# Unread matrix products in more idle gaps of TensorE, and the first half's rows of an attention loaded quad by quad

## The reference

```python
x = x + 0.5 * L0_ffn(layernorm(x))    # three trees of 16 leaves give q, k, v; then softmax(q k) v
x = x + L0_attn(layernorm(x))         # 16 causal heads of 8, rope, alibi
x = x + 0.5 * L0_ffn(layernorm(x))
x = x + 0.5 * L1_ffn(layernorm(x))    # 8 experts, top 2, and a shared one
x = x + L1_attn(layernorm(x))         # a state space block: conv, scan over 16 states, gate
x = x + 0.5 * L1_ffn(layernorm(x))
```

## Time and profile before

| | |
|---|---|
| median of three runs | 1326.98 us (1323.32, 1326.98, 1327.03) |
| profiled execution | 1324.17 us, its span 1322.4 us |
| PE busy | 1220.3 us, 92% of the span, 6083 products |
| DVE, ACT, POOL busy | 906.3, 641.6 and 241.4 us (69%, 49%, 18%) |
| chain that ended last | PE 72%, DVE 11%, ACT 9% |
| mean granted clock of PE | 0.989 of full speed |

### The profile page before, as it was taken

How to read it: one execution, slowest core, us unless ns; L and a number is a source line. 1 busy time by engine, 2 the same in 40 slices (tenths; PEclk the granted TensorE clock), 3 DMA queues, 4 the chain that set the end, 5 groups by cost and what they waited for, 6 DMA issues and landing times.

```text
span 1322.4 us, 17165 instructions
## 1 busy us (share of the span) xinstructions
PE 1220.3 (92%) x6083; PEld 784.8 (59%) x6132; DVE 906.3 (69%) x1754; ACT 641.6 (49%) x1188; POOL 241.4 (18%) x205
## 2 busy tenths in 40 slices
PE   5998788899899989899999969889998998999998
PEld 3676444567666555566667744346776665555665
DVE  6755867455467698986765677664555677889765
ACT  4544354544422597952234325454433227979222
POOL 3000100000020084751000010000000102938210
PEclk9999899999999999999999999999999999999999
DMA  6212220000101030320100032200001011212220
GB/s 231 57 33 80 56 76 19 2 1 1 64 1 64 4 118 23 116 81 1 73 25 1 24 89 54 63 3 0 1 1 64 16 50 58 81 58 80 65 72 9
DMA packets 33365, 63.27 MB, mean 48 GB/s; under 512 B 4384, under 2 KB 20096, under 8 KB 33088
## 3 DMA queue, kind: packets, MB, share of 16 engines
q1 hardware_dynamic: 33280, 62.17, 15.0%
HBM read 54.23 MB, written 8.45 MB: 47 GB/s over the span
## 4 chain that ended last, share of the span: by engine, by line
PE 72%; DVE 11%; ACT 9%; issue 3%; POOL 2%; DMA 2%; SPq 1%; another core or an unknown queue 0%; DVEq 0%; POOLq 0%; ACTq 0%
PE bank L1543 13%; PE bank L1545 13%; PE bank L1544 13%; PE bank L1722 9%; PE bank L1552 5%; DVE a_mx L1426 3%; ACT n_part L1093 3%; PE bank L1877 3%; PE bank L1621 3%; ACT n_da L1085 2%; PE bank L1787 2%; PE bank L1692 2%; POOL n_hc L840 2%; PE bank L1758 2%; PE bank L1826 1%
## 5 line engine op out<-in xcount | busy, mean ns | idle before, releaser
L1270 DVE SCALAR_TENSOR_TENSOR f_hl<-bank,f_hh 128x512 fp32r<-128x512 f32 x192 | 131.9, 689 | 130.4 <-ACT f_hh L914 129.6
L914 ACT ACTIVATE f_hh<-bank 128x512 fp32r<-128x512 f32 x192 | 115.0, 599 | 188.1 <-PE bank L1621 149.2
L980 ACT ACTIVATE m_sl<-bank 128x512 f32<-128x512 f32 x144 | 86.2, 599 | 235.4 <-PE bank L1545 233.4
L840 POOL TENSOR_TENSOR n_hc<-n_h,n_cs 128x512 f32<-128x512 f32 x128 | 160.7, 1287 | 35.3 <-DVE n_h L1514 31.1
L1543 PE MATMUL bank<-xT_h,mw_h 128*128 128x512 f32 x288 | 161.2, 560 | 3.5 <-DVEq L537 2.7
L1514 DVE TENSOR_TENSOR_SCAN n_h<-n_da,bank 128x512 f32<-128x512 f32 x128 | 149.1, 1206 | 5.1 <-PE bank L1552 2.3
L1722 PE MATMUL bank<-m_h,mw 128*128 128x512 f32 x288 | 145.6, 594 | 0.0
L1337 DVE TENSOR_TENSOR m_t<-m_sl,bank 128x512 f32<-128x512 f32 x128 | 87.9, 687 | 78.7 <-PE bank L1545 77.3
L1426 DVE TENSOR_REDUCE a_mx<-bank 128x1 f32<-128x384 f32 (+3 forms) x176 | 106.0, 638 | 39.8 <-PE bank L1828 37.4
L771 POOL TENSOR_TENSOR small<-small,half 128x4 f32<-128x4 f32 (+1 forms) x24 | 26.8, 1115 | 577.3 <-DVE small L1176 577.3
L1877 PE MATMUL bank<-n_hc,ident 128*128 128x512 f32 x256 | 131.0, 599 | 0.2
(11 more groups left out here) (248 smaller groups left out, 2331.1 us busy)
## 6 DMA issues: line engine op xcount, KB each, us to landing
n_cs<-c_dram SPq DMA_DIRECT2D x32, 512.0 KB, 3.6
m_c<-comb_dram SPq DMA_DIRECT2D x28, 512.0 KB, 5.2
stage_fw<-in_fw_dram SPq DMA_DIRECT2D x6, 512.0 KB, 6.4
stack_dram<-R SPq DMA_DIRECT2D x16, 192.0 KB, 2.8
w_stage<-in_mw_dram SPq DMA_DIRECT2D x9, 256.0 KB, 2.7
stack_dram<-R SPq DMA_DIRECT2D x16, 128.0 KB, 2.6
a_q<-stack_dram SPq DMA_DIRECT2D x4, 512.0 KB, 5.3
a_k<-stack_dram SPq DMA_DIRECT2D x8, 256.0 KB, 4.7
```

Source lines behind the costliest of these rows:

```text
L840: n_hcs.by(nc.gpsimd.tensor_tensor(n_hc[:, i % 4, :], n_h[:, i % 4, :], n_cs[:, j % C_RING, i // 2 % 2, :], ALU.mult))
L1270: f_lo.by(V.scalar_tensor_tensor(f_h[1][:, i % 4, :], bank[:, i % 3, :], 0.0, f_h[0][:, i % 4, :].bitcast(F32), ALU.max, ALU.subtract))
```

## The change

`keep_busy` gets the bank as an argument. `attend` gets a table: ahead of an item of the tail it makes that many unread products, into bank 1. `mha` makes unread products ahead of three jobs of the pair's first list. And the groups of rows become four, one for each quad, so that quads 0 and 1 are loaded and waited for by themselves.

```diff
+TAIL_IDLE = {("turn", 1): 7, ("turn", 2): 7, ("turn", 3): 3, ("weigh", 3): 7}
+FIRST_IDLE = {NS1 + 3: 3, NS1 + 5: 6, NS1 + 6: 15}
...
-        a_ldq = [sig(f"a_ldq_{n}", "mha", 1, 16) for n in range(3)]
-        a_ldk = [sig(f"a_ldk_{n}", "mha", 2, 16) for n in range(3)]
+        a_ldq = [sig(f"a_ldq_{n}", "mha", 1, 16) for n in range(QUADS)]
+        a_ldk = [sig(f"a_ldk_{n}", "mha", 2, 16) for n in range(QUADS)]
...
-                    for n in range(3):
+                    for n in range(QUADS):
                         sp.wait_ge(a_ldq[n].sem, a_ldq[n].at(k - 1, 0))
...
-                first, count = ((0, 4), (4, 2), (6, 2))[n]
+                first, count = 2 * n, 2
...
                         sp.wait_ge(unit_done, done_before(u))
-                        head_rows_in(k, 1)
                         head_rows_in(k, 2)
+                        head_rows_in(k, 3)
...
                             head_rows_in(k + 1, 0)
+                            head_rows_in(k + 1, 1)
...
                             sp.wait_ge(a_s2.sem, a_s2.at(k, 3 * STEPS_4 - 1))
-                            head_rows_in(k + 1, 1)
+                            head_rows_in(k + 1, 2)
...
                             sp.wait_ge(a_s2.sem, a_s2.at(k - 1, NS2 - 1))
-                            head_rows_in(k, 2)
+                            head_rows_in(k, 3)
...
                     head_rows_in(k, 0)
+                    head_rows_in(k, 1)
...
-                    attend(k, [item for at in sorted(ATTEND_AT) for item in ATTEND_AT[at]])
+                    attend(k, [item for at in sorted(ATTEND_AT) for item in ATTEND_AT[at]], TAIL_IDLE)
...
-            def attend(k, items):
+            def attend(k, items, idle={}):
                 for what, qt in items:
+                    keep_busy(idle.get((what, qt), 0), 1)
...
-                    for job, x, which in HEADS_PLAN[-1]:
+                    for n, (job, x, which) in enumerate(HEADS_PLAN[-1]):
+                        keep_busy(FIRST_IDLE.get(n, 0), 1)
                         head_job(k, job, which)
...
-                pe.wait_ge(a_fill.sem, a_fill.at(k // 2, 1 if n == 0 else 3))
+                pe.wait_ge(a_fill.sem, a_fill.at(k // 2, 1 if n < 2 else 3))
...
-                    if n % NS1 == 0 and quad != 1:
-                        rows_of_quads(k, max(quad - 1, 0))
+                    if n % NS1 == 0:
+                        rows_of_quads(k, quad)
...
-            def keep_busy(count):
+            def keep_busy(count, b=6):
 
                 for _ in range(count):
-                    mm(bank[:, 6, 0:3 * P], identb, flat(cbf[:]), start=True, stop=True)
+                    mm(bank[:, b, 0:3 * P], identb, flat(cbf[:]), start=True, stop=True)
```

## The result

| | before | changed |
|---|---|---|
| median, 12 runs each, same chip | 1325.76 us (1323.29 to 1327.03) | 1327.84 us (1325.44 to 1330.43) |
| ratio to before | | 1.0017, 95% interval 1.0009 to 1.0025 |
| profiled execution, its span | 1324.17, 1322.4 us | 1330.16, 1328.4 us |
| mean granted clock of PE | 0.989 | 0.996 |

The changed kernel is 2.1 us slower: inside the range I gave and within 0.3%, but on the slower side, where I had forecast 0.8 us less than the median of three then shown (1326.98). The profiled executions lie further apart (6.0 us), since before's is a low one of its runs and the changed kernel's a high one. What follows takes places and mechanisms from the profiles, and total times from the medians.

A forecast was written before the change was run, and what follows sets the result against it. Bound: PE's clock is nearly full, and tails are full chains with nothing beside them. 1324.17 + 7.6 − 0.5 − 2.4 − 2.4 − 1.7 = 1324.8, plus 1.4: median 1326.2 us, no change; range 1319.5 to 1331.

The forecast's parts named there:

- the tails: Four tails: products ahead of turn 1, turn 3 and weigh 3 lengthen the path 1.9 us per tail, +7.6 us.
- The clock behind the fourth tail: Low-clock stretch behind the fourth tail: with products in the gaps before it the clock holds, −0.5 us.
- the beginnings: Beginning of the pairs' attention, twice: products fit the idle gaps at no cost and the clock holds, −2.4 us.
- Rival C: The clock falls despite the products at both beginnings and second halves, tails' 7.6 against loads' 2.4: 1330.8 us; chance 0.12.
- the loads' −2.4 us: First slots of both second halves: smaller key loads by quads land 1.0 and 1.4 us earlier, −2.4 us.
- the clock's −1.7: Second halves: with a shorter gap ahead of the first slot, the clock holds in one of the two, −1.7 us.
- rival D: Second halves: the rule on transposes decides and the clock falls in both, 1327.9 us; chance 0.15.
- Rival A: Clock holds in both second halves, slots start right behind the turn, beginnings give back more: median 1321.7 us; chance 0.22.
- the step to the median: From the profiled execution, 2.8 us below the median shown, half of that added: 1324.8 + 1.4 = 1326.2 us.

The follow-up runs named there:

- the trace of the 14: The changed kernel with 14 unread products ahead of turn 1 and no others in the tails: 1327.62 us, 1.0003 of the kernel before.
- the run with 30: The changed kernel with 30 small unread products put ahead of PE's first job: 1326.61 us, 1.0001 of the kernel before.
- the run with 108: The changed kernel with 108 small unread products put ahead of PE's first job: 1324.87 us, 0.9997 of the kernel before.
- the run with 60: The changed kernel with 60 small unread products put ahead of PE's first job: 1325.57 us, 1.0000 of the kernel before.
- the rows-only run: The kernel before with only the first half's rows loaded by quads, both product tables empty: 1321.14 us, 0.9960 of the kernel before.

## Why the prediction was right and wrong

**Right: the tails.** The product's price (0.161 by the trace of the 14, 0.162 taken), what is hidden (ahead of turn 2) and what is not (1.15 us ahead of turn 1, 0.47 ahead of turn 3, 0.28 ahead of weigh 3), and the sum: 1.7 to 1.9 us per tail, 7.2 us for four, 7.6 taken. The clock behind the fourth tail gave 0.36 for 0.5.

**Right: the beginnings.** The gaps took the products without cost, the clock held, and 2.7 us came back in the profile (2.4 taken), 3.2 in the run of that part alone (1.8 to 4.4 by its interval). Rival C's first half is out.

**Which steps failed.** The two steps at the second halves: the loads' −2.4 us and the clock's −1.7. Together they gave −1.6 and −1.4 us in the two profiles of the changed kernel, not −4.1. And a term that the sum doesn't have, a late write in the state stage, cost 0.9 and 0.6 us in them.

**Wrong: "I take one of the two: −1.7 us".** The clock fell in both second halves of the changed kernel, in both profiles of it. That was rival D's outcome, 1327.9, and the median came out at 1327.84. The number fits, and that is luck in part: its reason is not shown, and it takes the loads' −2.4 as given, which did not come in full. The Trainium skill (TensorE: Matmul & The Clock Gate, part 4, PE-mode transpose) would have it that the turn in the gap doesn't count. At the beginnings of attention, gaps of 0.6 to 2.8 us filled with nothing but transposes kept the clock at 1.00 exactly as products did, so in this kernel, for fp32 blocks of 128 x 128, the rule is not borne out; bf16 transposes were not tried. Nor does the length of the wait decide: with 1.47 us ahead of the slot the clock held in one run, with 0.59 (first pair, fourteen ahead of turn 1) and 0.32 us (second pair, no tail products) it fell. With the gap left as it is, the clock held in 7 of the 28 second halves of 14 profiles; with products in it, in all 6 of 3 profiles. My one in two was too high, and what decides stays open. Rival A needed a held clock and slots right behind the turn in both second halves. Only two versions with the gap filled showed that (slots 0.65 to 0.82 us behind turn 3's start).

**Wrong: the loads' −2.4 us, and nothing for where the new instructions put the fetches.** I looked at who waits for SyncE's queue and for PE, and at no one who waits for the DMA engines behind them. The loads' gain was sized right for where nothing disturbs it. With quads 0 and 1 in one group, the first slot started 2.5 us behind turn 3 in the mean of the 7 cases without a late last write (1.94 to 2.93); with a group each, 1.2 in the mean of 15 (0.67 to 2.28): 1.3 us a time, where I had taken 1.2. With a late last write it was 2.0 in the mean of 5 (1.68 to 2.35), and most of the gain was gone.

Two places are late in both profiles of the changed kernel and not in those with 60 and 108 products ahead: the first pair's head rows (2.38 and 2.95 us for the last write, and 1.1 to 2.0 us of the stage) and the state stage at 1180.5 (0.9 and 0.6). They make 2.1 and 2.5 us. The 1.76 us at 809.9 stand in one of the two profiles alone, so the median can't rest on them. Shifting the fetches by 30, 60 or 108 small products took the changed kernel from 1.0017 and 1.0023 to 1.0001, 1.0000 and 0.9997, 2 to 3 us, on other chips than the unshifted kernel's repeat but each time against the kernel before on the same one. The shifted kernels lie 7.2 to 7.7 us above the version without tail products, which is what the tails cost. That the shift as a whole brings about 2 us is shown. That it does so through these two writes fits the size, and isn't shown to the end: the run with 30 kept a slow first pair and had a late write in another state stage, the run with 108 kept a late write in the second pair, and both were about as fast as the run with 60. In all three the clock held in at least one second half, and it is open whether the shift did that or chance.

**The missing addition.** The parts alone make −3.2 us, the whole +2.1. About 2 to 3 of these 5.3 us go with the place of the fetches. The rest lies within what the parts' intervals (1.8, 1.7 and 1.3 us to either side) leave open; the rows-only run is the one whose median its profile doesn't explain.

**Half right: the step to the median.** I added 1.4 us because the profiled execution looked lucky. Later medians of the kernel before were 1325.8 to 1326.7, 1.6 to 2.5 above it. But that step is also where the forecast of a gain came from. The sum itself had the changed kernel 0.6 us above the execution it started from (1324.8 against 1324.17); 1326.2 was a gain only beside a median of three, and against the 1325.76 of twelve runs it is a loss of 0.4. A difference of 0.8 us was less than that median could carry.

## What to carry to other kernels

Unread products are free only in idle time that the trace shows as a wait on PE itself: place each against its own wait, and check the row for one. Here half of the tails' products stood where PE had none, and leaving them out turns a loss of 2 us into a gain of 9 (0.9932 of before). And when parts of a change don't add up by a few us in a kernel whose stages hang on small writes through DRAM, look for the instruction queues in the DMA view beside these writes, and shift them once, with instructions at an idle place, before believing either sum.

## What the runs showed that I had not expected

The last 64 KB write of head rows took 1.37 to 1.40 us to release the next loads in all 27 profiled cases in which no 16 KB fetch lay at it, and 2.38, 2.43, 2.54, 2.82, 2.92, 2.95 and 2.96 us in the seven in which one began between 0.2 us before the query load and 0.7 us behind it (counted from the query load's issue to the key loads'). The state stage's 64 KB write repeats it: 1.61 to 1.63 us until the next load in 60 of 68 cases, and 2.3 to 2.9 us in the eight in which such a fetch began 0.07 to 0.45 us behind it. What a late write costs depends on who waits: at the second of a pair's two it was 0.9, 0.6 and 0.9 us, and at the first, where the kernel before had one too (459.0), it made a lasting difference of 0.3 us at most. The 12 KB writes of maxima are less regular: 1.37 us in most, 1.8 to 3.5 with a fetch near them, but some fetches beside them cost nothing (809.91 in the repeated changed kernel), and right behind the loads of a second half they took 1.4 to 3.3 us without any fetch.
